# First attention layer of a graph network: GpSimd waits for a pair's node times before its second four gathers, VectorE forms the last pair's weighted values before its next product

## The chip, the core and the metric

The kernel runs on one core of a Trainium2 chip. The metric is the time of one execution on the device, in microseconds (us), as the median of several runs. The engines are TensorE (PE in the profile; PEld is its weight load), VectorE (DVE), ScalarE (ACT), GpSimd (POOL) and SyncE (SP). They run their own instruction streams and meet only at semaphores.

## What is computed

The reference runs four layers over a graph with 3125 nodes and 100,000 edges, each followed by a residual sum and a layer norm. The change touches the first one alone, an attention over edges:

```
q, k, v = x@Wq+bq, x@Wk+bk, x@Wv+bv          # 8 heads of 32
time_diff = edge_time - node_time[dst]
time_features = stack([sign(time_diff), log1p(abs(time_diff)/3600)])
scores = einsum('ehd,ehd->eh', q[dst], k[src]) * scale + time_features @ Wt + bt
alpha = softmax(scores, axis=0)              # over all edges
out = segment_sum(alpha[..., None] * v[src], dst) @ Wo + bo
```

## The kernel before

Edges are sorted by destination into 220 macros of 512 edges (4 tiles of 128), each of which belongs to one bucket of 128 destination nodes. The layer works in 110 turns; turn t handles the pair of macros mA = 2t and mB = 2t+1, and finishes the pair before it, zA = mA-2 and zB = mB-2. No scheduler reorders anything: each engine runs its instructions in the order in which its function is written, and the semaphores named below do the rest.

- GpSimd (`pool`, L943) issues four indirect gathers for each macro (`gather`, L937: k and v rows of 128 edges, 512 floats each, into the buffer `gat`, which holds four macros). Gathers of macro m wait on `s_pv` for the weighted values of macro m-4, whose buffer they take. Between the gathers stand 7 scattered writes of edge records for a later layer (`rec_s`, L485): 3 behind the gathers of mA, 4 behind those of mB.
- TensorE (`tensor`) does for each turn: the weighted sums of the pair before (`sums`, L999, on `s_pv`, signals `s_sum`); then, once VectorE has made the pair's one-hots (`s_oh`), transposes of them (L972); once ScalarE has copied these (L1022), the node times (`node_times`, L981, signals `s_tx`) and the queries of each edge, first of mA, then of mB (`queries`, L990, signals `s_q`).
- VectorE (`turn`) does: the product of queries and gathered keys of mA (`multiply`, L1081, which waits for `s_q` and for the gathers), the weighted values of zA and zB (`weight_values`, L1093, two instructions, which wait for `s_p`, ScalarE's exponentials, and signal `s_pv`), the reduction (`scores`, L1086), product and reduction of mB, then the time term, the one-hots of the next pair (L1075; these wait on `s_sum` for the sums of zA and zB), the running maximum by a chain of small instructions, and last the time terms of the next pair (`node_time_scores`, L1115 to L1129), which begin with a wait on `s_tx`.

So a pair's one-hots, node times and queries are made in the turn ahead of it; the gathers of mA and mB of the next turn too.

Of the kernel before, what the change touches and what calls it, by code (L numbers as in the profile page):

```python
# [99 lines left out]
def bcast(ap, axis, shape):  # L100
    return ap.unsqueeze(axis).to_broadcast(shape)


def gnn_kernel(nc, io, out):
    ctx = ExitStack()
    with ctx:
# [3 lines left out]
        def sem(name):  # L110
            return ctx.enter_context(nc.semaphore(name))
# [44 lines left out]
        def S(name):  # L156
            if name not in sems:
                sems[name] = sem(name)
            return sems[name]
# [693 lines left out]
        def all_landed(e, totals):  # L853
            for u, n in enumerate(totals):
                if n:
                    e.wait_ge(s_gather[u], n)
# [15 lines left out]
        def attention_in_pairs(table):  # L872
# [6 lines left out]
            s_oh, s_tr, s_oht, s_tx, s_td, s_ln = (sem(f"a0_{n}") for n in ("oh", "tr", "oht", "tx", "td", "ln"))  # L879
# [38 lines left out]
            def have_records(e, t, first, first_at, rest, rest_at):  # L918
                if t == 0:
                    e.wait_ge(first, first_at)  # L920
                if PQ * (t + 1) > FIRST >= PQ * t:
                    e.wait_ge(rest, rest_at)

            def landed(e, m):
                e.wait_ge(s_gather[m % U], gathered[m % U] + 16 * Q * (m // U + 1))

            def bucket(e, m):
                return e.value_load(jmap["d"][0:1, m:m + 1], min_val=0, max_val=NB - 1)


            def gather(e, m):
                if m >= U:
                    e.wait_ge(s_pv, m - U + 1)
                e.sem_inc(S("s_gp"), 1)
                for q in range(Q):
                    at = Q * m + q
                    e.indirect_dma_start(  # L937
                        out=gat[:, m % U, q, :], out_offset=None, in_=table,
                        in_offset=bass.IndirectOffsetOnAxis(ap=all_d[:, at, 0:1].bitcast(I32), axis=0),
                    ).then_inc(s_gather[m % U], 16)  # L940

            def pool(e):
                write, half = by_source["write"], by_source["half"]  # L943
                for g in range(EARLY):
                    write(e, g)
                for t in range(2):
                    have_records(e, t, S("s_first_d"), 16, S("s_rest_d"), 16)
                    gather(e, 2 * t)
                    gather(e, 2 * t + 1)
                for t in range(2):  # L950
                    write(e, t + EARLY)
                for t in range(2, NP):
                    have_records(e, t, S("s_first_d"), 16, S("s_rest_d"), 16)
                    g = t + EARLY
                    gather(e, 2 * t)
                    if g < NP:
                        write(e, g, range(0, half // 2))
                    gather(e, 2 * t + 1)
                    if g < NP:
                        write(e, g, range(half // 2, half))  # L960
                all_landed(e, every_gather)
# [110 lines left out]
            def one_hots(e, m):  # L1072
                if m >= U:
                    e.wait_ge(s_sum, m - U + 1)
                V.tensor_tensor(oh[:, m % U, :, :], bcast(iota[:, :], 1, [P, Q, P]),  # L1075
                                bcast(all_d[:, Q * m:Q * m + Q, 1], 2, [P, Q, P]), ALU.is_equal).then_inc(s_oh, 1)

            def multiply(e, m):
                e.wait_ge(s_q, m + 1)
                landed(e, m)  # L1080
                V.tensor_tensor(prod[m % 2], psQ[m % 2], gat[:, m % U, :, 0:D], ALU.mult).then_inc(s_prod, 1)  # L1081

            def scores(c, e, m):
                e.wait_ge(s_prod, m + 1)
                u = m % 2
                return c(V.tensor_reduce(sc[:, u * Q * H:(u + 1) * Q * H],  # L1086
                                         prod[u].rearrange("p (n c) -> p n c", c=DH), AX.X, ALU.add))

            def weight_values(e, m):
                e.wait_ge(s_p, m // 2 + 1)  # L1090
                pw = pvb[:, m % 2, :, :].rearrange("p q (h c) -> p q h c", c=HC)
                gv = gat[:, m % U, :, D:2 * D].rearrange("p q (h c) -> p q h c", c=DH)
                V.tensor_tensor(pw[:, :, :, 0:DH], gv, bcast(by_tile(psP[:, m % 2, :]), 3, [P, Q, H, DH]),  # L1093
                                ALU.mult).then_inc(s_pv, 1)
# [4 lines left out]
            def rescale(c, e, t, j):  # L1099
                e.wait_ge(s_ef, t + 1)  # L1100
                if t:
                    e.wait_ge(s_flush, 2 * t)
                return c(V.tensor_tensor(by_head(j), by_head(j), bcast(ff, 2, [P, H, HC]), ALU.mult))

            def add_sums(e, m, j):
                e.wait_ge(s_sum, m + 1)
                V.tensor_tensor(by_head(j), by_head(j), psO[m % 2].rearrange("p (h c) -> p h c", c=HC), ALU.add)\
                    .then_inc(s_flush, 1)

            def keep_maximum(c, t, j):  # L1110
                return c(move(m_run[:, bass.ds(j, 1), :].rearrange("p a h -> p (a h)"), mn[t % 2]))
# [19 lines left out]
            def turn(c, e, t):  # L1131
                mA, mB = 2 * t, 2 * t + 1
                zA, zB = mA - 2, mB - 2
                has_z, has_next = t > 0, t + 1 < NP
                multiply(e, mA)
                if has_z:
                    weight_values(e, zA)
                    weight_values(e, zB)
                    jA, jB = bucket(e, zA), bucket(e, zB)
                k_a = scores(c, e, mA)  # L1140
                multiply(e, mB)
                if has_z:
                    k_r = rescale(c, e, t - 1, jA)
                k_b = scores(c, e, mB)
                e.wait_ge(s_ln, t + 1)
                k = c(V.tensor_tensor(by_tile(t2), bcast(ln, 2, all_heads), bcast(w1, 1, all_heads), ALU.mult))
                if has_next:
                    have_records(e, t + 1, S("s_first_d"), 16, S("s_rest_d"), 16)
                    one_hots(e, mA + 2)
                c.wait(k)  # L1150
                k = c(V.tensor_tensor(t1, t1, t2, ALU.add))
                if has_z:
                    c.wait(k_r)
                    add_sums(e, zA, jA)
                c.wait(k)
                k = c(V.scalar_tensor_tensor(sc, sc, DH ** -0.5, t1, ALU.mult, ALU.add))
                if has_next:
                    one_hots(e, mB + 2)
                c.wait(k)
                k = c(V.tensor_reduce(mq32[:, 0:H], sc.rearrange("p (t h) -> p h t", h=H), AX.X, ALU.max))  # L1160
                if has_z:
                    e.wait_ge(s_flush, zA + 1)
                    add_sums(e, zB, jB)
                    keep_maximum(c, t - 1, jA)
                c.wait(k)
                k = c(V.transpose(mq32_t, mq32))
                c.wait(k)
                k = c(V.tensor_reduce(by_block[:, 0:1], mq32_t, AX.X, ALU.max))
                if has_z:
                    keep_maximum(c, t - 1, jB)  # L1170
                c.wait(k)
                for n in range(1, 4):
                    k = c(move(by_block[0:32, n:n + 1], by_block[32 * n:32 * n + 32, 0:1]))
                c.wait(k)
                k = c(V.tensor_reduce(mr, by_block[0:32, :], AX.X, ALU.max))
                c.wait(k)
                k = c(move(top32[0:32, :], mr.to_broadcast([32, 32])))
                c.wait(k)
                k = c(V.transpose(top32_t[0:32, :], top32[0:32, :]))
                c.wait(k)  # L1180
                for n in range(1, 4):
                    k = c(move(top32_t[32 * n:32 * n + 32, 0:H], top32_t[0:32, 0:H]))
                c.wait(k)
                k = c(V.tensor_tensor(mn[t % 2], mn[1 - t % 2], top32_t[:, 0:H], ALU.max))
                c.wait(k)
                c(V.tensor_tensor(by_tile(sm), by_tile(sc), bcast(mn[t % 2], 1, all_heads), ALU.subtract))
                V.tensor_tensor(dd, mn[1 - t % 2], mn[t % 2], ALU.subtract).then_inc(s_f, 1)
                if has_next:
                    node_time_scores(c, e, t + 1)
# [996 lines left out]
```

## Time and profile before

| | us |
|---|---|
| median of 3 runs | 9226.23 (9218.38 to 9244.98) |
| the profiled execution, its own time | 9166.33 |
| its span, first to last instruction | 9164.3 |
| TensorE busy | 5696.0 |
| GpSimd busy | 5730.8 |
| VectorE busy | 5469.0 |
| ScalarE busy | 1950.7 |

Busy shares of the whole span say little here, since the kernel has four layers with different limits. The changed layer is read by itself: its turns lie between 1210.8 and 3971 us of the span.

### The profile page before, as it was taken

Reading aid. Unit: us, or ns where it says so; the run is one execution under the profiler, and the core shown is the slowest. Engines: PE = TensorE matmul, PEld = TensorE weight load, DVE = VectorE, ACT = ScalarE, POOL = GpSimd, SP = SyncE. Lnnn points to the kernel's source line nnn. Section 1 sums busy time; section 2 is a strip of 40 time slices with the busy share of each in tenths; the row PEclk is TensorE's granted clock in tenths of the full one; section 3 lists DMA queues with packets and bytes.
Section 4 is the critical chain, followed back from the end, with each engine's and each line's share of the span. In section 5 each row is a group of like instructions: output and inputs, shape, how many; then the busy total and the mean of one; then the engine's idle time right before and its main releaser. Section 6 shows DMA issues by size and latency. Waiting matters only on the chain. (4 is left out here: it accounts for less than half of the span.)

```text
span 9164.3 us, 105731 instructions
## 1 busy us (share of the span) xinstructions
PE 5696.0 (62%) x27368; PEld 3956.0 (43%) x27369; DVE 5469.0 (60%) x12757; ACT 1950.7 (21%) x5292; POOL 5730.8 (63%) x5534
## 2 busy tenths in 40 slices
PE   2121134444544444459999997899999997555555
PEld 0010023333333333347777765566666664333333
DVE  4100045555554555558999987899999997222224
ACT  0000011111111111123333332444444442000000
POOL 5777755666555555547777762666666665666663
PEclk6555566777767666779999997999999998777776
DMA  1000033333333233323333342444444444333334
GB/s 67 1 10 11 10 90 83 93 91 92 87 87 88 82 85 84 85 58 85 88 88 86 86 82 50 123 126 123 124 125 124 124 124 99 92 92 92 92 92 52
DMA packets 379540, 773.51 MB, mean 84 GB/s; under 512 B 163698, under 2 KB 200284, under 8 KB 378716
## 3 DMA queue, kind: packets, MB, share of 16 engines
q0 software_dynamic: 277632, 706.83, 29.8%
q1 hardware_dynamic: 101724, 64.57, 2.3%
q8 instruction: 73, 1.20, 0.1%
q14 instruction: 111, 0.91, 0.0%
HBM read 730.97 MB, written 40.07 MB: 84 GB/s over the span
## 5 line engine op out<-in xcount | busy, mean ns | idle before, releaser
L937 POOL DMA_INDIRECT gat<-kv,all_d x880 | 867.0, 985 | 896.9 <-DVE big L1093 648.4
L1734 POOL DMA_INDIRECT gat<-y,rec_sb_s x892 | 1018.9, 1142 | 436.3 <-issue 284.8
L1271 POOL DMA_INDIRECT gat<-kv,rec_sb_s x900 | 864.2, 960 | 414.6 <-issue 313.8
L2001 POOL DMA_INDIRECT gat<-x,all_d x880 | 838.5, 953 | 446.9 <-issue 245.2
L2014 PE MATMUL ps<-gat,oh 128*128 128x256 f32 x1760 | 659.3, 544 | 644.7 <-issue 378.3
L1466 DVE TENSOR_REDUCE small<-ps 128x2 f32<-128x1024 f32 x884 | 1042.3, 1217 | 4.8 <-PE ps L1334 3.8
L434 POOL DMA_INDIRECT rec_d<-small x784 | 813.2, 1037 | 335.6 <-issue 261.0
L485 POOL DMA_INDIRECT rec_s<-acc,by_src x770 | 762.7, 991 | 273.7 <-issue 236.1
L999 PE MATMUL ps<-big,oh 128*128 128x264 f32 x1760 | 581.4, 500 | 545.6 <-DVE big L1093 520.1
L1775 PE MATMUL ps<-big,oh 128*128 128x256 f32 x3520 | 908.3, 390 | 0.0
L2014 PEld LDWEIGHTS ps<-gat,oh 128*128 128x128 f32 x1760 | 469.1, 278 | 834.5 <-issue 704.9
L999 PEld LDWEIGHTS ps<-big,oh 128*128 128x128 f32 x1760 | 436.9, 254 | 686.9 <-DVE big L1093 558.9
L1775 PEld LDWEIGHTS ps<-big,oh 128*128 128x128 f32 x3520 | 648.6, 194 | 101.2 <-issue 0.4
L2035 DVE TENSOR_TENSOR acc<-acc,ps 128x256 f32 x220 | 92.6, 421 | 963.5 <-remote 603.3
L972 PE MATMUL ps<-work,oh 128*128 128x128 bf16 x880 | 103.8, 253 | 863.1 <-DVE oh L1075 746.3
L1281 POOL TENSOR_TENSOR big<-gat,big 128x1024 f32<-128x1024 f32 x221 | 435.4, 1970 | 259.3 <-ACT big L1404 255.5
L990 PE MATMUL ps<-qz,work 128*128 x1760 | 589.5, 508 | 0.0
L1022 ACT ACTIVATE work<-ps 128x1024 f32<-128x1024 bf16 x110 | 112.7, 1024 | 2016.1 <-PE ps L972 1315.4
L1331 PE MATMUL ps<-wts,work 128*128 128x512 bf16 x1772 | 531.1, 381 | 0.2
L1334 PE MATMUL ps<-wts,small 128*128 128x512 bf16 x1772 | 528.4, 380 | 0.0
L990 PEld LDWEIGHTS ps<-qz,work 128*128 128x128 f32 x1760 | 454.3, 265 | 91.6
L972 PEld LDWEIGHTS ps<-work,oh 128*128 128x128 bf16 x880 | 61.6, 110 | 923.0 <-DVE oh L1075 789.2
(275 smaller groups left out, 11800.7 us busy)
## 6 DMA issues: line engine op xcount, KB each, us to landing
gat<-kv,rec_sb_s POOLq DMA_INDIRECT x900
rec_sb_s<-rec_s SPq DMA_DIRECT2D x448, 32.0 KB
gat<-y,rec_sb_s POOLq DMA_INDIRECT x892
gat<-kv,all_d POOLq DMA_INDIRECT x880
gat<-x,all_d POOLq DMA_INDIRECT x880
rec_d<-small POOLq DMA_INDIRECT x784
rec_s<-acc,by_src POOLq DMA_INDIRECT x770
rec_s<-gat SPq DMA_DIRECT2D x4, 1808.0 KB, 17.4
```

Of the source, the lines that this page charges most:

```text
L434: e.indirect_dma_start(out=recs["d"], out_offset=bass.IndirectOffsetOnAxis(ap=pring[:, h * RH + t:h * RH + t + 1], axis=0), in_=rr[:, h, t ...
L485: e.indirect_dma_start(out=recs["s"], out_offset=bass.IndirectOffsetOnAxis(ap=by_src[:, 2, at:at + 1].bitcast(I32), axis=0), in_=buffer(r) ...
L937: e.indirect_dma_start(out=gat[:, m % U, q, :], out_offset=None, in_=table, in_offset=bass.IndirectOffsetOnAxis(ap=all_d[:, at, 0:1].bitca ...
L990: last = T.matmul(psQ[m % 2][:, q * D:(q + 1) * D], oht[:, n * P:(n + 1) * P], qz[:, bass.ds(j, 1), :], start=True, stop=True)
L999: last = T.matmul(psO[m % 2], oh[:, m % U, q, :], pvb[:, m % 2, q, :], start=(q == 0), stop=(q == Q - 1))
L1271: e.indirect_dma_start(out=gat[:, m.u, q, :], out_offset=None, in_=table, in_offset=bass.IndirectOffsetOnAxis(ap=r_sb[:, m.u, q, 0:1].bitc ...
L1331: T.matmul(to[:, n, :], bigI, nh[m.u], start=True, stop=False)
L1466: V.tensor_reduce(mx[:, 2 * pair:2 * pair + 2], psH[pair % 2], AX.X, ALU.max).then_inc(s_hr, 1)
L1734: e.indirect_dma_start(out=rows_y[m.u][:, q, :], out_offset=None, in_=y1, in_offset=bass.IndirectOffsetOnAxis(ap=r_sb[:, m.u, q, 0:1].bitc ...
L1775: ins = T.matmul(to, oh[:, m.u, q, :], rows_m[m.v][:, q, part], start=(q == 0), stop=(q == Q - 1))
L2001: e.indirect_dma_start(out=gat[:, m % U, q, 0:D], out_offset=None, in_=x3, in_offset=bass.IndirectOffsetOnAxis(ap=all_d[:, t, 0:1].bitcast ...
L2014: last = T.matmul(ps[:, 5 + m % 2, 0:D], oh[:, m % U, q, :], gat[:, m % U, q, 0:D], start=(q == 0), stop=(q == Q - 1))
```

## The change

GpSimd gets one more wait in each turn from t = 2: ahead of the gathers of macro 2t+1 it waits for TensorE's node times of pair t (`s_tx` at t+1). VectorE's two `weight_values` of the pair before, with the two loads of their bucket numbers, stand ahead of the product of mA instead of behind it.

```diff
@@ pool(e)
                     gather(e, 2 * t)
                     if g < NP:
                         write(e, g, range(0, half // 2))
+                    e.wait_ge(s_tx, t + 1)
                     gather(e, 2 * t + 1)
                     if g < NP:
                         write(e, g, range(half // 2, half))
@@ turn(c, e, t)
                 has_z, has_next = t > 0, t + 1 < NP
-                multiply(e, mA)
                 if has_z:
                     weight_values(e, zA)
                     weight_values(e, zB)
                     jA, jB = bucket(e, zA), bucket(e, zB)
+                multiply(e, mA)
                 k_a = scores(c, e, mA)
```

GpSimd's instructions of one turn before, from the gathers of mA on (`a0_pv` is `s_pv`):

```order
L937 DMA gat<-kv,all_d 128x512 [waits a0_pv]
L937 DMA gat<-kv,all_d 128x512 x3
L485 DMA rec_s<-acc,by_src 115712x16 [waits s_rows_s]
L485 DMA rec_s<-acc,by_src 115712x16 x2
L937 DMA gat<-kv,all_d 128x512 [waits a0_pv]
L937 DMA gat<-kv,all_d 128x512 x3
L485 DMA rec_s<-acc,by_src 115712x16 x4
```

The second four gathers in the changed kernel, and what follows:

```order
L937 DMA gat<-kv,all_d 128x512 [waits a0_tx,a0_pv]
L937 DMA gat<-kv,all_d 128x512 x3
L485 DMA rec_s<-acc,by_src 115712x16 x4
```

Nothing is moved here; the first of the second four waits for `s_tx` too, and the three gathers and four writes behind it stand behind that wait.

VectorE before, from the last instruction of a pair's time terms into the next turn (`a0_q` is `s_q`, `a0_p` is `s_p`, `gathered0` counts landed gathers):

```order
L1129 TENSOR_TENSOR small<-small,acc 128x64 [waits a0_chain]
L1081 TENSOR_TENSOR big<-ps,gat 128x1024 [waits gathered0,a0_q]
L1093 TENSOR_TENSOR big<-gat,ps 128x32x32 [waits a0_p] x2
L928 TENSOR_LOAD jmap_d
L928 ISA x2
L928 TENSOR_LOAD jmap_d
L928 ISA x2
L1086 TENSOR_REDUCE small<-big 128x32 [waits a0_prod]
```

The same place in the changed kernel, whose lines from here on are numbered one higher:

```order
L1130 TENSOR_TENSOR small<-small,acc 128x64 [waits a0_chain]
L1094 TENSOR_TENSOR big<-gat,ps 128x32x32 [waits a0_p] x2
L928 TENSOR_LOAD jmap_d
L928 ISA x2
L928 TENSOR_LOAD jmap_d
L928 ISA x2
L1082 TENSOR_TENSOR big<-ps,gat 128x1024 [waits gathered0,a0_q]
L1087 TENSOR_REDUCE small<-big 128x32 [waits a0_prod]
```

The weighted values no longer stand behind the wait for the queries; they follow the time terms directly.

## Rows read from the trace of the kernel before

**Rows 1.** The page: its first line, and the group of the gathers.

```profile
span 9164.3 us, 105731 instructions
...
L937 POOL DMA_INDIRECT gat<-kv,all_d x880 | 867.0, 985 | 896.9 <-DVE big L1093 648.4
```

**Rows 2.** Line L1081: all products of mA, and the idle time before L1081.

```profile
L1081 DVE TENSOR_TENSOR big<-ps,gat x110: 1216/1225/1226, 1210.8 to 3957.2; 128x1024 f32<-128x1024 f32 x110
...
  remote: 641.9, 95
```

**Rows 3.** Waits in 1240:3972, us in total, times, longest.

```profile
POOL gat L937 <- DVE big L1093: 648.4, 80, 15.1
...
DVE big L1081 <- remote: 372.9, 60, 13.8
DVE oh L1075 <- remote: 299.6, 43, 11.2
```

**Rows 4.** Timeline of one turn: start, us, instruction [idle before it, releaser].

```profile
2001.03 1.23 DVE L1081 TENSOR_TENSOR big<-ps,gat 128x1024 f32<-128x1024 f32 x1 [5.98 <-remote]
2002.17 2.34 DVE L1093 TENSOR_TENSOR big<-gat,ps 128x1024 f32<-128x1024 f32 x2
...
2004.20 0.98 POOL L937 DMA_INDIRECT gat<-kv,all_d  x1 [4.55 <-DVE big L1093]
...
2012.26 0.39 PE L981 MATMUL ps<-rows,work 128*128 x8 [1.22 <-issue]
...
2012.54 3.71 PE L990 MATMUL ps<-qz,work 128*128 x16
...
2013.38 0.98 POOL L937 DMA_INDIRECT gat<-kv,all_d  x1 [0.31 <-issue]
...
2016.23 0.18 DVE L1115 TENSOR_REDUCE small<-ps 128x8 f32<-128x24 f32 x1 [2.31 <-remote]
...
2022.37 0.97 POOL L485 DMA_INDIRECT rec_s<-acc,by_src  x1 [0.30 <-issue]
2024.70 1.23 DVE L1081 TENSOR_TENSOR big<-ps,gat 128x1024 f32<-128x1024 f32 x1 [6.82 <-remote]
...
2029.23 1.21 DVE L1081 TENSOR_TENSOR work<-ps,gat 128x1024 f32<-128x1024 f32 x1
```

**Rows 5.** The same turn in slices: the end of the second gathers' data.

```profile
2019.00:2020.50 1.50, 0.00 (x0) 0.00 (x0) 0.00 (x0) 0.12 (x1) 1.20 (x2) 0.50 0.62 178
2020.50:2022.00 1.50, 0.00 (x0) 0.00 (x0) 0.00 (x0) 0.00 (x0) 1.20 (x2) 0.50 0.04 8
```

**Rows 6.** Timeline of a turn in which GpSimd did not pause.

```profile
3207.66 6.64 PE L990 MATMUL ps<-qz,work 128*128 x16
...
3215.99 1.23 DVE L1081 TENSOR_TENSOR big<-ps,gat 128x1024 f32<-128x1024 f32 x1 [5.32 <-remote]
...
3218.39 6.51 PE L999 MATMUL ps<-big,oh 128*128 128x264 f32 x16 [4.09 <-DVE big L1093]
3219.16 0.98 POOL L937 DMA_INDIRECT gat<-kv,all_d  x1 [0.37 <-issue]
...
3230.07 1.22 DVE L1081 TENSOR_TENSOR work<-ps,gat 128x1024 f32<-128x1024 f32 x1 [9.46 <-remote]
...
3237.04 0.97 POOL L485 DMA_INDIRECT rec_s<-acc,by_src  x1 [0.30 <-issue]
3241.96 0.69 DVE L1075 TENSOR_TENSOR oh<-iota,all_d 128x512 f32<-128x512 f32 x1 [9.07 <-remote]
...
3249.85 1.23 DVE L1081 TENSOR_TENSOR big<-ps,gat 128x1024 f32<-128x1024 f32 x1 [1.13 <-PE ps L990]
```

**Rows 7.** Timeline of one of the shortest even turns.

```profile
1264.77 1.23 DVE L1081 TENSOR_TENSOR big<-ps,gat 128x1024 f32<-128x1024 f32 x1 [6.85 <-remote]
...
1286.08 0.97 POOL L485 DMA_INDIRECT rec_s<-acc,by_src  x1 [0.30 <-issue]
1286.31 1.23 DVE L1081 TENSOR_TENSOR big<-ps,gat 128x1024 f32<-128x1024 f32 x1 [6.82 <-remote]
...
1289.47 0.98 POOL L937 DMA_INDIRECT gat<-kv,all_d  x1 [2.42 <-issue]
```

## The prediction

> **What bounds the layer now.** I first read the line of the product of mA, since it stands once in each turn. It ran 110 times from 1210.8 to 3957.2 us [rows 2], so 109 turns took 2746.4 us, 25.2 us each. The layer is 30% of the span [rows 1]; nothing outside it is touched. Then the waits: no engine is full. GpSimd waits 648 us for VectorE's weighted values, VectorE waits 373 us ahead of product A and 300 us ahead of the one-hots for something that the profile only calls remote, that is, a semaphore whose raiser it doesn't find [rows 3]; over both products it is 642 us [rows 2].
>
> What that is shows in the timeline of one turn [rows 4]. The reader is to see four things there. TensorE's queries are over at 2012.54 + 3.71 = 2016.25, but product A starts at 2024.70, 8.45 us later. Its gathers were issued from 2004.20 on and can't be meant: even the second four, issued from 2013.38 on, have moved their data by 2020.50, where the DMA share falls from 0.62 to 0.04 [rows 5]. GpSimd's last record write ends at 2022.37 + 0.97 = 2023.34, 1.36 us before the product starts. And the node times too: L981 ends at 2012.65, but L1115, which waits for them, starts at 2016.23, 3.6 us later. So TensorE's signals arrive late while GpSimd is issuing, and come through around the time when it stops. How a pause matters is seen in a turn without one [rows 6]: query A was through at 3215.99 while GpSimd was still issuing, the weighted values followed at once, and GpSimd went on after 0.37 us instead of pausing. Then product B waited until 3230.07 (queries were over at 3214.30), and the one-hots until 3241.96, though the sums were over at 3218.39 + 6.51 = 3224.90: 17.1 us late, and 3.95 us after GpSimd's last write (3237.04 + 0.97 = 3238.01). After that long pause the queries came at once (idle 1.13, releaser PE). That turn lasted 3249.85 - 3215.99 = 33.9 us. The even turns are 23.7 us [rows 4] or 1286.31 - 1264.77 = 21.5 us [rows 7]; the last have the shorter pause, 2.42 us. The signals early in a run of GpSimd are prompt in all these turns: in [rows 4] the node times, 8.5 us into the run that began at 2004.20, are the first that is late.
>
> I read the bound so: GpSimd's run of 15 issues takes 2023.34 - 2004.20 = 19.14 us; a turn is that, plus the pause in which the late signal gets through and product A (1.23), the first weighted value (half of 2.34) and 0.77 us to GpSimd's start follow: 2004.20 - 2001.03 = 3.17 us.
>
> **The change, part by part.** *VectorE's order.* The same instructions at the same lengths; nothing is added. The weighted values need ScalarE's exponentials, not the queries. In [rows 4] they would start some 1.6 us behind 2016.23 (eight instructions of about 0.2), at 2017.8, instead of 2025.9. So GpSimd's next four gathers and TensorE's sums are free about 8 us sooner, and GpSimd's pause at this place (4.55 us in [rows 4]) goes. The two bucket loads move ahead of product A; they run on the sequencer beside 2.34 us of weighted values and cost nothing. If product A found its queries there, 2.34 us would be added ahead of it, but 2.34 us fall away behind it: from product A to the node times it is now 2012.26 - 2001.03 = 11.2 us, then 8.9.
>
> *GpSimd's wait.* Behind it stand four gathers and four writes (9.96 us, 2013.38 to 2023.34), and behind these the next first four and three writes (9.18 us). Who waits for them: product B for the gathers; nobody near for the writes. Count a turn from r, when the node times' signal is through:
> - GpSimd starts at r + 0.8 and issues 19.14 us: until r + 19.9. The next first four have what they need (weighted values at r + 1.6 + 2.3). Then it waits for the next node times.
> - The queries end 3.6 us behind the node times. They fall in the first microseconds of GpSimd's new run, where signals were prompt. Product A at r + 4.0 (behind time terms and weighted values).
> - Product B needs the second gathers: issued from r + 0.8 until r + 5.6, their data there 2.3 us later (2018.2 to 2020.5, by [rows 4, 5]), r + 7.9. Without that it would start 2.2 us behind product A (4.5 now, less 2.34), r + 6.2. So the wait costs VectorE 1.7 us.
> - The next node times are then done at r + 4.0 + 8.9 + 1.7 + 0.4 = r + 15.0, 5 us before GpSimd is done.
>
> So GpSimd is the bound, and the 1.7 us are hidden by those 5. The signal, though, falls 14 us into a run, where it is late. It came 1.36 us after the last write [rows 4], in the other turn 0.74 us before that write's end, 1287.05 less 1286.31 [rows 7]. The first gives r + 21.3; the second lets GpSimd go on without a gap, r + 19.2 at best. I take the middle, 20.6 with a short pause, for nine turns in ten, and for the tenth a long hold of 31 us (about that of the last rival): 0.9 x 20.6 + 0.1 x 31 = 21.6 us, practically that of [rows 7]. Gain: 109 x (25.2 - 21.6) = 392 us. The bounds: 109 x (25.2 - 20.3) = 534 us less with hardly a late signal, and what the rivals give upwards.
>
> The sum is made against one execution of 9166.33 us, 0.65% under the median of the runs shown and under the lowest of them; I take the difference from the median: 9226 - 392 = 8834 us. In a profile that would be a span near 8772.
>
> A rule that speaks against the wait: the Trainium skill, "DMA: Bandwidth & Descriptors", Rules for kernel authors, says to issue a DMA early and wait for it late, so that its fixed cost overlaps with compute. The change does the reverse. This case's trace agrees that it costs nothing only while there is slack.
>
> In rows, the delay is from 2013.38 to 2016.23 + 0.8 = 2017.0, 3.65 us. Product B at 2029.23 follows its predecessor without a wait, 8.7 us after the data were there [rows 4, 5]. If all 3.65 us reached the end of each turn, it would be 398 us more, 9624.
>
> **Rivals.**
> 1. *The pause is lost (slower).* Before, GpSimd paused at the wait for weighted values; now this never holds it, and if the node times' signal gets through before the run's end, it doesn't pause at all. Then what [rows 6] shows follows: the queries' signal held for the whole next run. A short turn of 17.5, then 2.4 + 19.1 of issuing, 4.0 until the signal is through, 8.9 to the node times: 34.4. Mean 26.0, so 109 x 0.8 = 87 us more, 9313. It decides where the signal comes more than 0.8 us before the last write's end. For it: in [rows 6] one came 2.8 us before the run's end. Against: here it's raised 3 us later in the run. If this alternates with the good pattern, (26.0 + 21.0) / 2 = 23.5, 9041. I give the whole pattern 0.10 and the mixture 0.14.
> 2. *Each turn's queries are held to the run's end (slower).* r + 19.9 + 1.4, then 8.9 + 0.4: 30.6 us, 9226 + 589 = 9815. For it: the queries in [rows 4] were. Against: they were raised 10 to 12 us into a run, now 1 to 4. 0.06, and 0.04 for the gathers' own delay (9624).
> 3. *The wait and the order do nothing.* If signals are late for another reason than GpSimd's issuing, queries 8.45 us late stay so and the turn stays within 23.7 to 25.2: 9063 to 9226. 0.06 for no change that can be told.
> 4. The forecast, turns of 20.3 to 23: 8692 to 8986, 0.60.
>
> **How the numbers follow.** No change means within 0.3%, 28 us, 9198 to 9254; less can't be told from it. Faster: 0.60 + 0.14 = 0.74; same 0.06; slower 0.10 + 0.06 + 0.04 = 0.20. The range reaches from 20.3 us for each turn, 8692, rounded to 8700, up to the whole pattern of rival 1, 9320; above it is about 0.10, below 0.03.
>
> **What will show it.** Right: products A some 21 us apart; the idle time ahead of L1082 falls from 642 to under 250 us; GpSimd's wait moves from L1093 to TensorE's L981 or "remote" ahead of the second gathers; sums (L1000) start before the next product A. Wrong: long waits (over 10 us) ahead of L1082 or L1076 with GpSimd's idle time before it under 1 us (rival 1); product A following the run's end in each turn (rival 2); product B waiting on the DMA of `gat` (the gathers' own delay). My weakest step is that a signal raised 14 us into a run comes around its end and that the short pause clears what's behind it.

## The result, and the profile after

| | before | after |
|---|---|---|
| median of 4 runs, us | 9228.77 (9218.38 to 9244.98) | 9153.20 (9146.88 to 9161.21) |
| profiled execution, own time, us | 9166.33 | 9146.88 |
| products of mA, first and last start, us | 1210.8 to 3957.2 | 1218.5 to 3749.6 |
| mean turn of the layer, us | 25.20 | 23.22 |

The ratio is 0.9914, with a 95% interval from 0.9893 to 0.9935: faster, by 0.9% and not by the 4.2% of the forecast. The page of the changed kernel, against [rows 1] (group, count | busy us, mean ns | idle before, main releaser):

```profile
span 9144.8 us, 105509 instructions
...
L937 POOL DMA_INDIRECT gat<-kv,all_d x880 | 874.1, 993 | 675.0 <-PE ps L982 298.4
```

The reader is to see that GpSimd still waits 675 us ahead of its gathers (897 before), now for the node times (L982) and no more for the weighted values. The products of queries and keys, against [rows 2]:

```profile
L1082 DVE TENSOR_TENSOR big<-ps,gat x110: 1212/1215/1225, 1218.5 to 3749.6; 128x1024 f32<-128x1024 f32 x110
...
  remote: 254.6, 33
  DMA gat<-kv,all_d: 207.5, 90
```

Waits for a late signal ("remote") fell from 642 to 255 us, and 208 us for the gathers' own data came in. 109 turns in 3749.6 - 1218.5 = 2531.1 us are 23.22 us each. The waits of the layer's stretch, against [rows 3] (who waits, for what: us in total, times, longest):

```profile
ACT work L1023 <- remote: 683.3, 42, 19.6
...
POOL gat L937 <- PE ps L982: 298.4, 45, 12.1
DVE small L1116 <- remote: 262.0, 58, 6.0
...
DVE work L1082 <- DMA gat<-kv,all_d: 191.6, 88, 4.7
...
DVE big L1082 <- remote: 165.9, 15, 15.1
```

The largest of them is on an engine that the prediction did not follow: ScalarE, ahead of its copy of the transposes (L1023). In the kernel before, the same line, one number lower there, was:

```profile
ACT work L1022 <- remote: 160.0, 6, 29.6
```

So the change itself brought this late signal. Counted from the traces, the copy started over 1 us late in 6 of 110 turns before and in 47 after. One ordinary turn, in which that is seen, against [rows 4] (start, us, instruction [idle before it, releaser]; "issue" is a wait for nothing that the profile shows):

```profile
2499.54 0.41 PE L982 MATMUL ps<-rows,work 128*128 x8 [8.29 <-ACT work L1023]
...
2499.98 0.18 DVE L1116 TENSOR_REDUCE small<-ps 128x8 f32<-128x24 f32 x1 [6.06 <-PE ps L982]
2500.80 0.97 POOL L937 DMA_INDIRECT gat<-kv,all_d  x1 [3.00 <-PE ps L982]
...
2503.83 1.22 DVE L1082 TENSOR_TENSOR big<-ps,gat 128x1024 f32<-128x1024 f32 x1
...
2508.42 1.22 DVE L1082 TENSOR_TENSOR work<-ps,gat 128x1024 f32<-128x1024 f32 x1 [2.13 <-DMA gat<-kv,all_d]
...
2513.13 0.40 PE L973 MATMUL ps<-work,oh 128*128 128x128 bf16 x4 [0.82 <-DVE oh L1076]
...
2517.95 1.02 ACT L1023 ACTIVATE work<-ps 128x1024 f32<-128x1024 bf16 x1 [14.98 <-remote]
...
2519.13 0.41 PE L982 MATMUL ps<-rows,work 128*128 x8 [5.60 <-issue]
2519.31 0.97 POOL L485 DMA_INDIRECT rec_s<-acc,by_src  x1 [0.30 <-issue]
...
2522.30 0.18 DVE L1116 TENSOR_REDUCE small<-ps 128x8 f32<-128x24 f32 x1 [5.92 <-remote]
2523.11 0.97 POOL L937 DMA_INDIRECT gat<-kv,all_d  x1 [2.83 <-remote]
```

With r = 2499.96, when the node times' signal is through: GpSimd starts at r + 0.84, product A at r + 3.9, product B at r + 8.5. The transposes end at 2513.53, but their copy starts 4.4 us later, so the next node times are done at 2519.54, r + 19.6 and not r + 15.0. They come through another 2.8 us later. The turn is 22.3 us. In another kind of turn GpSimd does not pause:

```profile
1588.58 0.41 PE L982 MATMUL ps<-rows,work 128*128 x8 [1.22 <-issue]
1588.85 5.54 PE L991 MATMUL ps<-qz,work 128*128 x16
...
1592.87 0.18 DVE L1116 TENSOR_REDUCE small<-ps 128x8 f32<-128x24 f32 x1 [2.86 <-remote]
...
1594.21 0.98 POOL L937 DMA_INDIRECT gat<-kv,all_d  x1 [0.30 <-issue]
...
1595.69 3.83 PE L1000 MATMUL ps<-big,oh 128*128 128x264 f32 x16 [1.30 <-DVE big L1094]
...
1611.85 1.23 DVE L1082 TENSOR_TENSOR big<-ps,gat 128x1024 f32<-128x1024 f32 x1 [15.08 <-remote]
...
1624.56 0.97 POOL L937 DMA_INDIRECT gat<-kv,all_d  x1 [11.53 <-PE ps L982]
```

The node times' signal was through 1.3 us before GpSimd needed it, so GpSimd went on after 0.30 us, and the signal of the queries of mA, over at about 1592.6, was held until 1611.85. TensorE had started the next sums (L1000) at 1595.69, so it was the signal that was late and not TensorE's queue. That turn took 1611.85 - 1577.37 = 34.5 us. There were 12 turns of 30 us or more (33.9 on average), 12 behind them of 17.7, and 85 others of 22.5: together 23.2.

**The rest of the difference lies in layers that the change does not touch.** In the profiled pair the layer gained 212 us (its gathers took 3954.2 - 1203.1 before, by the trace, and 3750.0 - 1211.1 after), the span only 19.5. The gathers of the second and third layer before (first and last start, us):

```profile
L1734 POOL DMA_INDIRECT gat<-y,rec_sb_s x892: 954/960/2096, 4097.6 to 5536.0; - x179
...
L1271 POOL DMA_INDIRECT gat<-kv,rec_sb_s x900: 945/952/1007, 5734.1 to 7690.3; - x180
```

And after:

```profile
L1735 POOL DMA_INDIRECT gat<-y,rec_sb_s x892: 951/957/2010, 3892.2 to 5446.3; - x179
...
L1272 POOL DMA_INDIRECT gat<-kv,rec_sb_s x900: 942/948/1065, 5638.6 to 7667.4; - x180
```

The second took 1554.1 us instead of 1438.4, the third 2028.8 instead of 1956.2, which is 188 us given back. The four timed runs of the changed kernel lie within 15 us, so the profiled one is no exception among them. E14 and E13 below show what that is worth as evidence against the change.

### The profile page after: what moved, and what is told of

It reads as the page before. It is cut to its first block and busy times, and to the rows that moved or that the text cites. A ratio compares the mean times of both kernels' runs of the same rounds, so it can differ in the third digit from the quotient of the medians.

```text
span 9144.8 us, 105509 instructions
## 1 busy us (share of the span) xinstructions
PE 5659.4 (62%) x27146; PEld 3925.1 (43%) x27369; DVE 5485.8 (60%) x12757; ACT 1936.3 (21%) x5292; POOL 5718.4 (63%) x5534
## 5 line engine op out<-in xcount | busy, mean ns | idle before, releaser
L1735 POOL DMA_INDIRECT gat<-y,rec_sb_s x892 | 996.9, 1118 | 573.9 <-DMA rec_sb_s<-rec_s 285.1
L1776 PEld LDWEIGHTS ps<-big,oh 128*128 128x128 f32 x3520 | 660.1, 198 | 105.7 <-issue 1.1
L991 PE MATMUL ps<-qz,work 128*128 x1760 | 642.9, 544 | 0.0
L1000 PE MATMUL ps<-big,oh 128*128 128x264 f32 x1760 | 459.2, 419 | 141.6 <-DVE big L1094 139.7
L991 PEld LDWEIGHTS ps<-qz,work 128*128 128x128 f32 x1760 | 492.6, 287 | 106.6
L1332 PE MATMUL ps<-wts,work 128*128 128x512 bf16 x1606 | 495.0, 381 | 9.4 <-issue 0.2
L1023 ACT ACTIVATE work<-ps 128x1024 f32<-128x1024 bf16 x110 | 112.6, 1023 | 1711.9 <-PE ps L973 684.4
L1000 PEld LDWEIGHTS ps<-big,oh 128*128 128x128 f32 x1760 | 359.8, 207 | 230.6 <-DVE big L1094 160.6
```

Of the source, the lines that this page charges most:

```text
L991: last = T.matmul(psQ[m % 2][:, q * D:(q + 1) * D], oht[:, n * P:(n + 1) * P], qz[:, bass.ds(j, 1), :], start=True, stop=True)
L1000: last = T.matmul(psO[m % 2], oh[:, m % U, q, :], pvb[:, m % 2, q, :], start=(q == 0), stop=(q == Q - 1))
L1735: e.indirect_dma_start(out=rows_y[m.u][:, q, :], out_offset=None, in_=y1, in_offset=bass.IndirectOffsetOnAxis(ap=r_sb[:, m.u, q, 0:1].bitc ...
L1776: ins = T.matmul(to, oh[:, m.u, q, :], rows_m[m.v][:, q, part], start=(q == 0), stop=(q == Q - 1))
```

## The experiments

They were run at five occasions, each with its own runs of the kernel before on the same chip. At the first two (E1 to E4, E9 to E12) the kernel before took 8207 us, at the others about 9200 us as in the table above. That was not planned. Kernels of the same code at different occasions have labels of their own. E5 to E8, the same four kernels as E9 to E12, have no result.

**E1 to E4: the parts, each alone.** E1 is the kernel before. E2 adds the wait alone, E3 makes VectorE's new order alone, E4 adds a wait in the same place that has long been met:

```diff
                     if g < NP:
                         write(e, g, range(0, half // 2))
+                    e.wait_ge(s_tx, t + 1)      # E2; in E4 it is t - 1; in E3 there is none
                     gather(e, 2 * t + 1)
```

> The kernel before once more, to see how far two loads of one program differ by layer. In the profile of before the turns of the first layer are 25.2 us, the gathers of the second layer span 1438 us and those of the third 1956 us; in the changed kernel these are 23.2 us, 1554 us and 2029 us. Theory A (the second and third layer differ with where or how a program is loaded, not with the change): this run can show the second layer near 1554 us or in between, and a span between 9150 and 9300 us. Theory B (the change itself slows the later layers): 1438 and 1956 us again, within 1%, and a span of 9164 us within 30.

> Only GpSimd's wait for the node times ahead of the second four gathers; VectorE's order as before. Theory 1 (the wait forces a pause in GpSimd's issuing, and the pause is what lets TensorE's late signals through): few turns over 30 us are left, and GpSimd pauses twice in a turn, at the node times and at the weighted values; turns of about 24 us, layer 1 shorter than before by 50 to 150 us. Theory 2 (the order of VectorE is what gains, since it frees GpSimd's first gathers early): turns of 25 to 28 us, layer 1 as before or longer by up to 300 us.

> Only VectorE's new order; GpSimd without the new wait. Theory 1: GpSimd now hardly ever pauses, its runs get longer than 19 us, and long waits (over 10 us) ahead of the products and the one-hots become the rule: turns of 26 to 31 us, layer 1 longer by 100 to 600 us. Theory 2: the turn falls to near GpSimd's 19.1 us of issuing, 20 to 22 us, and layer 1 is 350 to 550 us shorter than before.

> The kernel before with one more wait instruction at the same 108 places of GpSimd's program, for a count that was reached long before (node times of the pair before last), so that it never waits. It shifts GpSimd's code as the change does and does nothing else. If the shifted code slows the second and third layer (theory C), their gathers span about 1554 and 2029 us here too, with turns of layer 1 near 25 us and a time of about 9350 us. If not, they stay as in a run of the kernel before on the same chip, and the time is that of before within 0.3%.

The kernel before took 8206.91 us here (31 runs). Ratios to it, with intervals: E1 1.0003 (0.9993 to 1.0013), E2 0.9996 (0.9987 to 1.0006), E3 1.0006 (0.9996 to 1.0015), E4 0.9999 (0.9989 to 1.0009). No part does anything, and nothing expected of the late signals was there to be seen. The products of mA of E1:

```profile
L1081 DVE TENSOR_TENSOR big<-ps,gat x110: 1223/1225/1226, 1124.4 to 3268.4; 128x1024 f32<-128x1024 f32 x110
...
  DMA gat<-kv,all_d: 591.5, 195
```

The same code makes turns of (3268.4 - 1124.4) / 109 = 19.67 us, against 25.20, and no product waits for a late signal, though GpSimd issues as before. So its issuing alone does not make TensorE's signals late. A turn of it:

```profile
2206.83 0.98 POOL L937 DMA_INDIRECT gat<-kv,all_d  x1 [0.30 <-issue]
...
2219.07 0.61 PE L972 MATMUL ps<-work,oh 128*128 128x128 bf16 x4 [0.60 <-DVE oh L1075]
2219.71 1.02 ACT L1022 ACTIVATE work<-ps 128x1024 f32<-128x1024 bf16 x1 [13.34 <-PE ps L972]
...
2220.90 0.41 PE L981 MATMUL ps<-rows,work 128*128 x8 [1.22 <-ACT work L1022]
...
2226.54 0.98 POOL L937 DMA_INDIRECT gat<-kv,all_d  x1 [0.30 <-issue]
```

The transposes end at 2219.68 and their copy starts 0.03 us later, 12.9 us into a run of GpSimd's that never pauses: 2226.54 - 2206.83 = 19.71 us are its 15 issues and nothing else. So here GpSimd's issuing is the bound, and neither wait nor order can shorten it.

**E9 to E12: the change as a whole, and a later wait.** E9 is the changed kernel, E10 repeats E2, E11 repeats E3. E12 is the changed kernel with a wait for both queries of the pair, which TensorE makes behind the node times:

```diff
-                    e.wait_ge(s_tx, t + 1)
+                    e.wait_ge(s_q, 2 * t + 2)
                     gather(e, 2 * t + 1)
```

> The changed kernel once more. In the first comparison the kernel before took 9229 us; on the chip of the last four runs it took 8207 us, TensorE's signals were prompt, the turn was 19.7 us, and neither half of the change made a difference. Theory 1 (TensorE's signals are late only under some condition of the chip, and the change is worth something only there): where the kernel before takes near 8207 us, this one is the same within 0.2%, with turns of 19.7 us; where it takes near 9200 us, this one is 0.5 to 1.2% faster, with turns near 23 us. Theory 2 (the two halves together do what neither does alone): faster by 50 us or more on any chip.

> Only GpSimd's wait for the node times, once more. Where the kernel before takes near 8207 us: same, turns of 19.7 us (both theories). Where it takes near 9200 us: theory 1a (the wait's pause is what helps) few turns over 30 us, turns of about 24 us, 50 to 150 us less; theory 1b (the order helps) turns of 25 to 28 us, no gain.

> Only VectorE's new order, once more. Where the kernel before takes near 8207 us: same. Where it takes near 9200 us: theory 1a, turns of 26 us and more and a longer time, since GpSimd has hardly a pause; theory 1b, turns of 21 to 24 us and a gain of 100 us or more.

> The changed kernel, but GpSimd waits ahead of the second four gathers for both macros' queries of pair t (s_q at 2t+2) in place of the node times, which is 3.6 us of TensorE later. Then no signal of transposes, node times or queries is raised while GpSimd issues, only those of the sums. Where signals are prompt: by the sum of the prediction VectorE and TensorE are 5 us ahead of GpSimd in each turn, so 3.6 us later still fit and the turn stays near 19.7 us, at most 21.5; if that slack is smaller than worked out, the turn grows by the difference. Where signals are late: if a pause lets them through, the turn is 22 us or less and few exceed 30 us; if not, 25 us and more.

Again the kernel before took 8207.59 us (25 runs), and E9 was 1.0004 (0.9994 to 1.0014), E10 0.9997 (0.9988 to 1.0007), E11 1.0004 (0.9994 to 1.0013), E12 1.0175 (1.0158 to 1.0192). Where signals are prompt, the change is worth nothing, and the later wait costs: E12's turn was 20.86 us, E9's 19.66. E12's gathers and the idle time ahead of them:

```profile
L937 POOL DMA_INDIRECT gat<-kv,all_d x880: 942/952/1506, 1115.4 to 3401.9; - x176
...
  PE ps L991: 166.3, 106
```

166.3 / 106 is 1.57 us, 1.27 more than the 0.30 that lie between any two issues, and that is the turn's 1.20. In E9 the node times were ready by 2215.05 and GpSimd came to them at 2220.25, so the wait of the change had more than 4 us of slack, about the 5 of the prediction. The queries end over 5 us behind the node times, and use it up.

**E13: the kernel before, for the other layers.**

> One look at the kernel before, to find which condition the chip is in. If TensorE's lateness belongs to a chip or to a time (theory 1), it takes either near 8207 us with every signal prompt, or near 9200 us with signals up to 20 us late, and nothing in between; if it belongs to how a program happens to be loaded (theory 2), times between the two are as likely.

One run, 9185.99 us, beside 9252.07 for another execution of the same code: the late signals were back, with a turn of 25.02 us. Its second layer:

```profile
L1734 POOL DMA_INDIRECT gat<-y,rec_sb_s x892: 951/959/2056, 4082.4 to 5562.2; - x179
```

That is 1479.8 us where the first profile of the same code had 1438.4.

**E14 to E17: the four versions where signals are late.** E14 is the changed kernel, E15 the wait alone, E16 the order alone, E17 the changed kernel with the wait of E12.

> The changed kernel where the kernel before takes about 9200 us. Theory 1 (late signals from TensorE, which the change arranges better): 0.5 to 1.2% faster again, turns of the first layer near 23 us. If it was the load of a program and not the change: anything within 1% of before. The gathers of the second and third layer, 1554 and 2029 us in the first profile of the change against 1438 and 1956 us: if the change slows them, the same again; if they vary from run to run, other values.

> Only GpSimd's wait for the node times, where the kernel before takes about 9200 us. Theory 1a (the wait's pause is what helps): few turns over 30 us, turns of about 24 us, 50 to 150 us less. Theory 1b (the order helps): turns of 25 to 28 us, no gain.

> Only VectorE's new order, where the kernel before takes about 9200 us. Theory 1a: turns of 26 us and more and a longer time, since GpSimd has hardly a pause. Theory 1b: turns of 21 to 24 us and a gain of 100 us or more.

> The changed kernel with GpSimd waiting for both macros' queries instead of the node times ahead of the second four gathers, where the kernel before takes about 9200 us. Where signals are prompt it cost 1.2 us a turn (20.9 after 19.7). If a pause of GpSimd lets late signals through, the turn is now 22 us or less, few exceed 30 us, and the first layer is 100 us or more shorter than with the change. If not, turns of 23 us and more.

The kernel before took 9199.19 us (13 runs, 9126.75 to 9249.54).

| | median us | ratio, 95% interval | mean turn |
|---|---|---|---|
| E14, wait and order | 8999.75 | 0.9801 (0.9730 to 0.9872) | 23.66 |
| E15, wait alone | 8933.17 | 0.9730 (0.9658 to 0.9802) | 22.71 |
| E16, order alone | 9164.16 | 0.9969 (0.9934 to 1.0004) | 24.98 |
| E17, wait for the queries, order | 8846.55 | 0.9637 (0.9568 to 0.9707) | 21.98 |

The gain is the wait's. The order alone is not told from nothing, and beside the wait it seems to take some of the gain away (23.66 us against 22.71), though the intervals of E14 and E15 overlap. Against what was expected: E14 and E15 gained more (2.0% and 266 us, for 0.5 to 1.2% and 50 to 150 us), E17's first case came true, and E16 fits neither theory, neither slower nor a gain of 100 us. E14's second and third layer:

```profile
L1735 POOL DMA_INDIRECT gat<-y,rec_sb_s x892: 951/959/2052, 3937.5 to 5417.6; - x179
...
L1272 POOL DMA_INDIRECT gat<-kv,rec_sb_s x900: 942/948/1004, 5607.6 to 7561.3; - x180
```

1480.1 and 1953.7 us, with the changed kernel's own code; E13, without the change, had 1479.8. So the 188 us that the first pair of profiles gave back there do not come with the change.

E16 shows what the order does when nothing makes GpSimd pause. Its turns alternate: 50 took under 15 us (mostly 14.2) and 52 over 33 (mostly 35.8). A long one, from product A to product A, with the first issue behind it:

```profile
2240.93 1.22 DVE L1081 TENSOR_TENSOR big<-ps,gat 128x1024 f32<-128x1024 f32 x1
...
2246.42 0.98 POOL L937 DMA_INDIRECT gat<-kv,all_d  x1 [0.30 <-issue]
...
2268.96 0.69 DVE L1075 TENSOR_TENSOR oh<-iota,all_d 128x512 f32<-128x512 f32 x1 [8.48 <-remote]
...
2276.45 0.97 POOL L937 DMA_INDIRECT gat<-kv,all_d  x1 [11.21 <-DVE big L1093]
2276.68 1.22 DVE L1081 TENSOR_TENSOR big<-ps,gat 128x1024 f32<-128x1024 f32 x1
```

The weighted values free GpSimd early (it goes on at 2246.42 without a pause), the sums' signal is then held until 2268.96, and GpSimd stands for 11.2 us. That is rival 1's mechanism, in every second turn, and it eats what the order gives.

E17, the later wait, has its products' idle time in another place:

```profile
  DMA gat<-kv,all_d: 689.0, 111
  remote: 34.2, 16
```

Only 34 us of late signals are left of 255. ScalarE's copy never waits for a late one (683 us in the changed kernel; here it starts within 0.04 us of the transposes in every turn), and one turn alone is over 30 us. What the products wait for now is the gathers' own data, 6 us for each pair, but that lies beside GpSimd's issuing:

```profile
2586.06 0.97 POOL L937 DMA_INDIRECT gat<-kv,all_d  x1 [2.14 <-PE ps L991]
...
2593.55 1.23 DVE L1082 TENSOR_TENSOR work<-ps,gat 128x1024 f32<-128x1024 f32 x1 [5.94 <-DMA gat<-kv,all_d]
...
2598.91 1.02 ACT L1023 ACTIVATE work<-ps 128x1024 f32<-128x1024 bf16 x1 [15.30 <-PE ps L973]
...
2605.45 1.23 DVE L1082 TENSOR_TENSOR big<-ps,gat 128x1024 f32<-128x1024 f32 x1
...
2607.86 0.97 POOL L937 DMA_INDIRECT gat<-kv,all_d  x1 [2.44 <-PE ps L991]
```

A turn is 2607.86 - 2586.06 = 21.8 us: the 15 issues and a pause of 2.4. That is still 1.1 us more than E12's 20.86, the same code where signals are prompt.

**E18 and E19: the later wait without the order.** E18 is the kernel before with the wait of E12, E19 the same with a wait for the first query of the pair alone:

```diff
+                    e.wait_ge(s_q, 2 * t + 2)      # E19: 2 * t + 1
                     gather(e, 2 * t + 1)
```

> VectorE's order as before, and GpSimd waits for both macros' queries ahead of the second four gathers. Where signals are late, the change took 23.7 us a turn, the wait without the new order 22.7, and the change with the wait moved to the queries 22.0. If the new order costs by taking away GpSimd's pause at the weighted values (theory 1), this one has both pauses: 21 us a turn, below 8850 us. If the two pauses add up to more than they free (theory 2): 22 us and more. Where signals are prompt: theory 1 and 2 alike, a little over the 20.9 us of the same wait with the new order, since the second gathers land as late and the weighted values stand behind the product again.

> As the last one, but GpSimd waits for the queries of the first macro alone (s_q at 2t+1), 1.7 us of TensorE earlier. Where signals are late: between the wait for the node times (22.7 us) and the last kernel if the place of the pause grades the gain; about the last kernel's turn plus what a held second query costs, 22 to 24 us, if any signal left behind undoes it. Where signals are prompt: 19.7 to 20.5 us.

Beside 9190.85 us for the kernel before (7 runs), E18 took 8851.55 us, 0.9641 (0.9593 to 0.9688), and E19 8843.63, 0.9640 (0.9589 to 0.9690), with turns of 22.22 and 21.93 us. With the later wait the order makes no difference that can be told; of E18's two theories it is the second, that two pauses free no more than one. One added line, without the order, thus gives more than the whole change where signals are late. E19 wasn't run where they are prompt; by E12 the wait for both queries costs 1.75% there.

## Why the prediction was right in sign and wrong in size

Two steps failed. The order of VectorE was credited with a gain that it does not have, and the transposes' signal was taken as prompt at its new place, so that an ordinary turn was put at 20.6 us and measured 22.5. The rest of the difference in time lies outside the layer.

- **What bounds the layer.** Right for the executions with late signals: TensorE's signals come late while GpSimd issues, and an added pause of GpSimd shortens the turn. E15, E18 and E19, which only add a wait, take 2.3 to 3.1 us off the turn of E13, 25.02 us. With E1 the price of the late signals can be put at 25.20 - 19.67 = 5.5 us a turn, though those two profiles differ in the granted clock too. That a signal comes through when GpSimd stops is no rule: the one that released 1592.87 above came while GpSimd was issuing.
- **VectorE's order.** The prediction credited it with the pause of 4.55 us that it removes. Alone it gave 0.04 us a turn (E16 against E13), beside the wait nothing (E14, E15; E17, E18). That step failed. By the rows of E16 the pause had let signals through: without it they were held for the next run, in every second turn.
- **The count from r.** Right up to product B: r + 3.9 for r + 4.0, r + 8.5 for r + 7.9, and 2.1 us of waiting for gathers for 1.7. The next node times were done at r + 19.6, for r + 15.0. Here the sum missed 4.4 us between the transposes and ScalarE's copy, a signal of TensorE too, raised 12.7 us into the run. It was taken as prompt, though [rows 4] had a late one 8.5 us into the run. This step failed too.
- **The 20.6 us of an ordinary turn** are the mis-sized term. They measured 22.5, since the node times' signal is raised as GpSimd's run ends (r + 19.6 and r + 20.3), and comes through 2.8 us later. "Around its end" was the step named as the weakest. (The middle of the two cases given, r + 21.3 and r + 19.2, is r + 20.3; no row shows the 0.3 us that 20.6 adds.)
- **A tenth with a long hold.** The number was met by luck (12 turns of 109; the same code has 24 in E14). The price was too high: a pair of such a turn and the one behind it averages (33.9 + 17.7) / 2 = 25.8 us, near rival 1's 26.0, so the pairs add some 0.7 us to the mean turn and not 1.0. The whole miss in the layer, 23.2 for 21.6, is thus the ordinary turn's. E14, with 23.66 us, is near the mixture's 23.5.
- **The queries.** Prompt in most turns, as forecast: product A waited for a late signal 15 times. Rival 2 did not happen. Whether the 2.1 us of waiting for the second gathers reach the end of a turn no run here shows.
- **The sum.** In the layer 109 x (25.20 - 23.22) = 216 us were gained instead of 392. Of those the timed runs kept 76. The profiled pair has 188 us more in the second and third layer, and E14 does not show them: its third layer took 1953.7 us, as in every other profile where signals are late (1953.7 to 1958.0), and only that first profile of the change has 2028.8. Why was not measured, so the missing 140 us are placed, not explained.
- **Rival 3** (wait and order do nothing) is true where signals are prompt, but by another cause than it named. The traces before gave no sign that the same code could run so.

The Trainium skill, "DMA: Bandwidth & Descriptors", Rules for kernel authors, says to issue early and wait late. Where signals are prompt the trace of E12 agrees: later gathers cost 1.2 us a turn. Where they are late E17 does the reverse of the rule and gains 25.02 - 21.98 = 3.0 us a turn.

## What to carry to other kernels

Where a consumer starts long after its producer's modelled end, and the releaser is unknown, look at what another engine does in the gap and at its pauses: here GpSimd's idle time was no loss, and removing it gave nothing. Count every signal of the suspected kind around the whole loop, not only those at the change. And before tuning against such a wait, profile the same kernel at another occasion; the wait may not be there, and the cure (E12) may cost.

## What was not expected of the hardware

The same code took 8207 us at two occasions and about 9200 at the others. It is not the chip alone: the records of E9 and E18 name the same chip number, with 8207.59 and 9190.85 us for the kernel before.

In the first layer the traces show TensorE's signals as the difference. In the first profile of the changed kernel a copy starts 4.4 us behind the transposes, and over 1 us behind them in 47 turns; in E9, the same code, no copy starts more than 0.04 us behind them. The gathers (a median of 952 to 963 ns) and the products (1.22 us) last as long in both kinds, and the transposes are shorter where signals are late (253 against 305 ns each). The signals that the trace records come late from TensorE alone: in the first profile of the kernel before, those of the queries come at a median of 3.6 us behind their modelled end, those of the products and of the weighted values 0.01 us behind theirs.

These traces are also less complete. The page gives the median time from a gather's issue to its landing for E1, and has too few landings to give one for the first profile of the same code:

```profile
gat<-kv,all_d POOLq DMA_INDIRECT x880, 3.7
```

```profile
gat<-kv,all_d POOLq DMA_INDIRECT x880
```

That trace holds 68 of the 110 signals of the transposes, E1's all of them. Part of what is called "remote" can thus be a record that is missing. The late starts themselves are measured, but whether the recording has a part in them no run here shows.

The mean granted clock of the two executions of the kernel before was 0.826 (E1) and 0.792; whether that is cause or consequence is not shown. The gain of 5.5 us a turn is 603 us of the 957 between these two profiles. Most of the rest lies ahead of the layer (the first gather starts 86 us sooner in E1) and in the gathers of the other layers (91, 29 and 145 us).

The Trainium skill, "Perfetto Trace Analysis", Tensor Engine Instruction, says that the profiler only estimates TensorE's end. E1 shows the estimate to hold to 0.03 us there. Where signals are late no run checks it, but in the turn of 1588.58 above TensorE had started its next sums 16 us before the queries' signal came, which a wrong end of the queries would hardly allow. What makes the signals late, the load of the chip, where the program lies or the recording, no run here could set, and it stays open.
